# Two-layer decoder on one core: context work of layer 2 behind the first experts, sixteen early maxima, and half of the last sums on PE

## What is computed

```python
x = _layernorm(x + _L0_attn_ref(x, ...))             # ALiBi: 8 heads look back, 8 look forward
x = _layernorm(x + _L0_xattn_ref(x, ctx_768, ...))   # scores clipped to +-10000
x = _layernorm(x + _L0_ffn_ref(x, ...))              # top 2 of 8 gated experts, 704 wide
x = _layernorm(x + _L1_attn_ref(x, ...))             # full attention
x = _layernorm(x + _L1_xattn_ref(x, ctx_768, ...))   # k = ctx @ wk + bk, v = ctx @ wv + bv
x = _layernorm(x + _L1_ffn_ref(x, ...))              # causal latent attention, then top 2 of 8 experts, 512 wide
```

## Time and profile before

| | |
|---|---|
| median of 3 runs | 2091.39 us (2084.49 to 2094.41) |
| profiled execution | 2086.37 us |
| its span in the trace | 2084.6 us |
| PE busy | 1872.3 us (90%), 12192 matmuls |
| DVE busy | 1316.5 us (63%) |
| ACT busy | 1023.2 us (49%) |
| POOL busy | 518.6 us (25%) |
| TensorE's granted clock, mean | 0.94 of 2.4 GHz |

### The profile page before, as it was taken

The page is one execution under the profiler, slowest core; times in us unless marked ns, Lnnn a source line. Parts: engine busy times, 40 slices in busy tenths (PEclk is TensorE's granted clock), DMA queues, the critical chain, the costliest instruction groups (busy, mean ns, idle before and its releaser), DMA issues. The chain is left out here.

```text
span 2084.6 us, 35007 instructions
## 1 busy us (share of the span) xinstructions
PE 1872.3 (90%) x12192; PEld 1089.2 (52%) x12193; DVE 1316.5 (63%) x2305; ACT 1023.2 (49%) x1992; POOL 518.6 (25%) x869
## 2 busy tenths in 40 slices
PE   7899999797689999958999999987988999986992
PEld 4444445342679999934232222253453444476992
DVE  4688874698643333366888888556587888654114
ACT  3266666486212222243677777754643666632333
POOL 3211103333223332212000000222352101043551
PEclk9799999899789999988999999998998999977996
DMA  7554312520911111055221121055046234051224
GB/s 195 134 119 66 49 20 58 133 43 2 373 47 35 35 33 33 30 150 124 39 32 31 32 46 16 1 129 118 11 92 123 43 52 63 2 202 38 71 70 139
DMA packets 98874, 157.94 MB, mean 76 GB/s; under 512 B 31415, under 2 KB 78839, under 8 KB 93559
## 3 DMA queue, kind: packets, MB, share of 16 engines
q1 hardware_dynamic: 86898, 131.55, 27.4%
q0 software_dynamic: 7488, 20.46, 3.1%
q10 hardware_dynamic: 4352, 4.20, 0.6%
HBM read 110.44 MB, written 44.72 MB: 74 GB/s over the span
## 5 line engine op out<-in xcount | busy, mean ns | idle before, releaser
L1871 ACT ACTIVATE arena<-psum 128x512 f32<-128x512 f32 (+1 forms) x1120 | 578.3, 591 | 310.4 <-PE psum L1817 215.9
L1616 DVE TENSOR_REDUCE arena<-psum 128x1 f32<-128x1024 f32 (+7 forms) x384 | 431.0, 1159 | 92.1 <-PE psum L1574 56.7
L1817 PE MATMUL psum<-arena 99*128 99x512 bf16 (+7 forms) x1280 | 369.6, 352 | 8.7 <-DMA arena<-arena 6.3
L1574 PE MATMUL psum<-arena 96*128 96x512 bf16 (+7 forms) x1280 | 355.6, 361 | 15.1 <-SPq L2605 7.3
L2338 PEld LDWEIGHTS psum<-arena 128*128 128x128 f32 x2340 | 278.7, 195 | 7.4 <-ACT arena L2385 3.4
L2338 PE MATMUL psum<-arena 128*128 128x128 f32 x2340 | 280.0, 278 | 2.0 <-ACT arena L2385 1.4
L1835 PE MATMUL psum<-arena 128*32 128x512 f32 (+3 forms) x2560 | 280.7, 538 | 0.7 <-ACT arena L1871 0.7
L2431 DVE COPY arena<-arena 128x1536 f32 (+1 forms) x117 | 97.1, 830 | 287.1 <-PE psum L2338 284.3
L1602 DVE CUSTOM_DVE_ANT_0 arena<-psum,arena 128x1024 bf16<-128x1024 f32 (+3 forms) x224 | 217.4, 1020 | 49.1 <-PE psum L1574 48.9
L1817 PEld LDWEIGHTS psum<-arena 99*128 99x128 bf16 (+1 forms) x1280 | 120.4, 98 | 218.6 <-ACT arena L1871 122.4
L1574 PEld LDWEIGHTS psum<-arena 96*128 96x128 bf16 (+1 forms) x1280 | 109.6, 100 | 184.4 <-DVE arena L1616 47.4
(11 more groups left out here) (207 smaller groups left out, 2301.8 us busy)
## 6 DMA issues: line engine op xcount, KB each, us to landing
arena<-k_parts SPq DMA_DIRECT2D x144, 128.0 KB
q_halves<-arena SPq DMA_DIRECT2D x80, 192.0 KB, 2.9
arena<-q_halves SPq DMA_DIRECT2D x40, 384.0 KB, 4.8
arena<-in_L_ffn_up SPq DMA_DIRECT2D x8, 1408.0 KB, 17.1
arena<-q_halves SPq DMA_DIRECT2D x40, 256.0 KB, 5.3
k_parts<-arena SPq DMA_DIRECT2D x48, 192.0 KB, 3.1
arena<-in_L_ffn_down SPq DMA_DIRECT2D x9, 1024.0 KB, 13.4
arena<-y_rows SPq DMA_DIRECT2D x32, 256.0 KB, 4.0
```

The lines of the kernel that those rows point to most:

```text
L1574: last = nc.tensor.matmul(dst[:, base + lo:base + hi], q[0:rows, qh, h, qb % 4 * P:qb % 4 * P + P], k[0:rows, h, key0 + lo:key0 + hi], sta ...
L1616: nc.vector.tensor_reduce(dst, src, AX.X, ALU.max).then_inc(t("taken"), 1)
L1817: last = nc.tensor.matmul(b[:, at0:at0 + width], kk[0:rows, h, kb * P:kb * P + P], q[0:rows, qh, h, c0:c1], start=True, stop=diag is None)
L1871: nc.scalar.activation(probs[k % at.ahead][:, heads[0]:heads[-1] + 1, c0:c1], bank[st_bank[no % 3]][:, 0:len(heads) * width].rearrange("p ...
```

## The change

It has four parts, and a few costs of the planner.

1. The context part is divided by layer. `t0` keeps layer 1's; layer 2's (two of four key units, four of eight value units) moves into `t3`, with `ctx1_loads` (six DMAs of weights and biases) and two DMAs that load the context rows again. SP issues them behind the row loads of pair 5. PE takes this work after the transposes of pair 3. `vx` is cleared per layer by POOL (128x2048), no longer by DVE, which keeps two small writes. `vx` is stored one layer at a time: 1 MB at the start of `at0`, 1 MB at the start of `at1`.
2. `at0` has all 16 early maxima of job 0, with transpose, split and load, in `t0`.
3. In `xa0` and `xa1` POOL adds the bias of one row tile behind the split of each job. Costs in `CrossAttention.plan` go up, which changes the order of events; in `xa0` nine scores stand between the transpose of a job's maxima and that job's first score in most jobs, ten before.
4. In `t7` the sums of the odd pairs (1, 3, 5, 7) are made by PE in PSUM: per 128 tokens, identity times `x`, then diag(gate1) and diag(gate2) times the gathered rows, three f32 matmuls of 128x256. ACT makes the 16 diagonal tiles of 128x128. DVE takes these pairs' moments from PSUM and ACT normalises from there.

Its core (`@@` lines tell where; new lines of the small helpers that only pass the layer on are left out):

```diff
@@ task costs of a token stage (make_plan)
-                    task("SP", "cload", 0, 4.0, 3.0)
+                if layer is not None:
+                    task("SP", "cload", 0, 5.0, 5.0, ("load", 5))
...
-                        task("SP", "load", p, 1.0, 5.0 if p < 4 else 3.5, ("add", p - 4))
-                    task("DVE", "add", p, 0.75 if source == "proj" else 1.9, 0.15, ("prj", p), ("load", p),
-                         (normed if not norm else "norm", p - 4), ("more", p - 4))
-                    task("DVE", "moments", p, 1.25, 0.15, ("add", p), ("square", p - 4))
+                        task("SP", "load", p, 1.0, 2.8 + 1.4 * p if p < 4 else 5.0, ("add", p - 4), ("sum", p - 4))
+                    if final and p % 2:
+                        task("ACT", "diag", p, 0.9, 0.15)
+                        task("PE", "sum", p, 2.6, 0.2, ("diag", p), ("load", p))
+                        task("DVE", "moments", p, 1.25, 0.15, ("sum", p))
+                    else:
+                        task("DVE", "add", p, 0.75 if source == "proj" else 1.9, 0.15, ("prj", p), ("load", p),
+                             (normed if not norm else "norm", p - 4), ("more", p - 4))
+                        task("DVE", "moments", p, 1.25, 0.15, ("add", p), ("square", p - 4))
...
-                    free = ("att", n_pairs - 1), ("add", n_pairs - 1), ("cmove", 7), ("cbias", 3)
+                    free = ("att", n_pairs - 1), ("add", n_pairs - 1), *context_ends(layer)
...
             def load_rows(sp, p):
                 if p >= 4:
-                    sp.wait_ge(t("r"), p - 3)
+                    summed(sp, p - 4)
...
+            def row_of(u):
+                if on_pe(u // 2):
+                    return bank[u // 4][:, (u % 2) * D:(u % 2) * D + D]
+                return r_tok[:, u % TPB, :]
...
+            def act_diag(act, p):
+                for u in (2 * p, 2 * p + 1):
+                    for k in range(2):
+                        last = nc.scalar.activation(diag_of(u, k), ident, ACT.Copy, scale=gate_w[:, k, u:u + 1])
+                last.then_inc(t("diag"), 1)
...
+            def pe_sum(pe, p):
+                pe.wait_ge(t("diag"), p // 2 + 1)
+                pe.wait_ge(t(f"rows{p % 4}"), 32 * (p // 4 + 1))
+                for u in (2 * p, 2 * p + 1):
+                    nc.tensor.matmul(row_of(u), ident, x_tok[:, u, :], start=True, stop=False)
+                    for k in range(2):
+                        last = nc.tensor.matmul(row_of(u), diag_of(u, k), gathered[:, k, u % TPB, :],
+                                                start=False, stop=(k == 1))
+                last.then_inc(t("prj_ps"), 1)
...
@@ ContextPart
-            def tasks(self, task):
-                task("DVE", "cclear", 0, 4.5, 0.15)
-                for n in range(len(self.kunits)):
-                    task("PE", "ckey", n, 1.1, 0.2, ("cload", 0), ("cbias", n - 2))
+            def tasks(self, task, layer):
+                task("POOL", "czero", 0, 2.2, 0.2)
+                task("DVE", "cclear", 0, 1.5, 0.15, ("czero", 0))
+                for n in (2 * layer, 2 * layer + 1):
+                    task("PE", "ckey", n, 1.3, 0.2, ("cload", 0), ("trx", 3), ("cbias", n - 2))
...
-            def load(self, sp):
+            def load(self, sp, layer):
                 load_context_rows(sp)
-                load_weights(sp, self.wn)
+                if layer == 0:
+                    load_weights(sp, self.wn)
+                else:
+                    for dst, src in ctx1_loads:
+                        sp.dma_start(dst, src, allow_slow_non_contiguous=True).then_inc(sem(f"weights{self.wn}"), 16)
...
-                for l in range(2):
-                    sp.dma_start(vx_scr[l], self.vx[:, l].rearrange("p g b n w -> p (g b n w)"))\
-                        .then_inc(t("vstored"), 16)
...
+                sp.dma_start(vx_scr[l], self.vx[:, l].rearrange("p g b n w -> p (g b n w)"))\
+                    .then_inc(t("vstored"), 16)
...
+            def pool_zero(self, pool, l):
+                nc.gpsimd.memset(self.vx[:, l].rearrange("p g b n w -> p (g b n w)"), 0.0).then_inc(self.t("zero"), 1)
...
-                nc.vector.memset(vx.rearrange("p l g b n w -> p (l g b n w)"), 0.0).then_inc(t("zero"), 1)
...
@@ cross_attention_stage, pool_prog
                 for j in range(1, len(at.jobs)):
                     maxima.pool_split(pool, j)
-                if bias:
-                    add_bias(pool, *bias)
+                    if bias:
+                        add_bias(pool, *bias, (j - 1,) if j < NT - 1 else (j - 1, j))
...
@@ CrossAttention.plan
-                clips.append(on_dve(exps[no], 0.62))
+                clips.append(on_dve(exps[no], 0.7))
...
-                taken.append(on_dve(free["PE"] + 0.2, 0.75))
+                taken.append(on_dve(free["PE"] + 0.2, 0.8))
...
@@ the program
-        at0 = SelfAttention("at0", ("fwd", "bwd"), True, q_halves, k_scr, 8)
+        at0 = SelfAttention("at0", ("fwd", "bwd"), True, q_halves, k_scr)
...
-                     ("v", w["wv"], w["bv"])], w, following=at1)
-        self_attention_stage(at1, (5, W["t4"]["brow"]))
+                     ("v", w["wv"], w["bv"])], w, following=at1, layer=1)
+        self_attention_stage(at1, (5, W["t4"]["brow"]), lambda sp: context.store_values(sp, 1),
+                             rows_free=lambda eng: context.values_stored(eng, 1))
```

More of the change, by code:

```diff
@@ L445, in plan @@
                 free["PE"] = when + (0.25 if tile < HG else 0.5)
-                free["ACT"] = max(free["ACT"], free["PE"] + 0.2, pvs[2 * j - 5] if j > 2 else 0.0) + 0.59
+                free["ACT"] = max(free["ACT"], free["PE"] + 0.2, pvs[2 * j - 5] if j > 2 else 0.0) + (0.7 if kind == "F" else 0.61)
                 exps.append(free["ACT"])
@@ L744, in token_stage @@
         def token_stage(name, wn, source, norm, rms, outs, w, x_out=True, h_rows=None, final=False,
-                        early_sp=None, following=None, between_sp=None, next_weights=True, context=None):
+                        early_sp=None, following=None, between_sp=None, next_weights=True, layer=None):
             def t(n):
@@ L789, in make_plan @@
                 normed = "norm" if rms is None else "rms"
-                if context:
-                    task("SP", "cload", 0, 4.0, 3.0)
+                if layer is not None:
+                    task("SP", "cload", 0, 5.0, 5.0, ("load", 5))
                 for p in range(n_pairs if has_in else 0):
@@ L856, in make_plan @@
                         task("SP", "eload", 0, 1.6, 2.0, ("esplit", 0))
-                if context:
-                    context.tasks(task)
+                if layer is not None:
+                    context.tasks(task, layer)
                 return list_order(tasks)
@@ L862, in ring, with on_pe, summed @@
                 return slice(2 * (p % 4), 2 * (p % 4) + 2)
+            def on_pe(p):
+                return final and p % 2 == 1
+            def summed(eng, p):
+                if final:
+                    eng.wait_ge(t("prj_ps" if on_pe(p) else "r"), p // 2 + 1)
+                else:
+                    eng.wait_ge(t("r"), p + 1)
+            def row_of(u):
+                if on_pe(u // 2):
+                    return bank[u // 4][:, (u % 2) * D:(u % 2) * D + D]
+                return r_tok[:, u % TPB, :]
             def tiles(p):
@@ L934, in sp_prog @@
                     elif kind == "cload":
-                        context.load(sp)
+                        context.load(sp, layer)
                     elif kind == "cstore":
@@ L1002, in pool_prog @@
                         pool_add(pool, n)
+                    elif kind == "czero":
+                        context.pool_zero(pool, layer)
                     elif kind == "cthird":
@@ L1087, in act_prog @@
                         act_norm(act, n)
+                    elif kind == "diag":
+                        act_diag(act, n)
                     elif kind == "xts":
@@ L1099, in act_prog, with diag_of @@
                         context.act_second(act, n)
+            def diag_of(u, k):
+                at0 = rest_base + 128 * (4 * (u // 4) + 2 * (u % 2) + k)
+                return arena[:, at0:at0 + P]
+            def pe_sum(pe, p):
[7 more added lines that the diff above has]
+                last.then_inc(t("prj_ps"), 1)
             def pe_tra(pe, p):
@@ L1173, in banks_free @@
                     pe.wait_ge(t("r"), n_pairs)
-                if context:
-                    context.banks_free(pe)
+                if layer is not None:
+                    context.banks_free(pe, layer)
             def pe_prog(pe):
-                weights_ready(pe, wn)
+                if wn is not None:
+                    weights_ready(pe, wn)
                 for kind, n in plan.get("PE", []):
@@ L1183, in pe_prog @@
                         pe_prj(pe, n)
+                    elif kind == "sum":
+                        pe_sum(pe, n)
                     elif kind == "trx":
```

(24 more changed lines are left out.)

73 lines of the change are left out of this document (44 added, 29 removed).

## The result

| | before | changed |
|---|---|---|
| median, us (runs) | 2091.39 (11) | 2078.8 (11) |
| ratio, 95% interval | | 0.9948 (0.9935 to 0.9961) |
| profiled execution, its span | 2086.4, 2084.6 | 2080.0, 2077.8 |
| PE, DVE, ACT, POOL busy | 1872, 1317, 1023, 519 | 1884, 1300, 1029, 520 |

The change gained 12.6 us of the forecast 24 by the medians, 10.9 by the ratio (8.2 to 13.6). Two single runs of some 3,700 to 3,800 us, one here and one among the experiments, are disturbed executions and stand in no ratio. The two traces differ by 6.8 us only, so part of the 12.6 is not in this pair. For that reason the stages are compared over all traces made, each from one barrier to the next. "Same stage" counts the versions of the changed kernel whose instructions are the same in that stage (for `xa0` and `xa1` those with the changed kernel's order and spread adds).

A forecast was written before the change was run, and what follows sets the result against it. PE bounded `t0`, PE and DVE `xa0`, DVE `t7`; `at0`'s start waited for a DMA. -6 -12 -4 +4.5 -4 = -21.5 gave 2064.9 us from the profile, 2069.9 against the median; taken 2067, range 2050 to 2081.

The forecast's parts named there:

- `t0`, -6: In `t0`, half of PE's context work leaves (-9.1), eight maxima units and a transpose come; the stage ends 6 us earlier.
- the wait for the group's data: In `t0`, early maxima units may stand before their keys land: a wait of up to 3 us, leaving -3.
- `at0`, -12: Start of `at0`: between 15 us gained by an earlier first score and 6.5 to 11.5 by job 2's earlier maxima.
- the start of `at0` is given back: Rival: job 2 waits in full and `t0`'s early units wait for keys; -3 and -7, 2075 us, chance 0.17.
- `xa0`, -4: In `xa0`, -9.5 at the end from spreading POOL's adds, +5.9 in the loop from a slower pace.
- a sign of being wrong: Wrong if `xa0` lengthens, `t3` grows by over 9, or `at0` begins early but ends where it ended.
- The end: End of `xa0`: with two adds instead of sixteen there, the 8.42 us PE wait behind a clip shrinks; about -9.5.
- the pace: Loop of `xa0`: a job takes 7.6 us against 7.15, +0.45 over 13 jobs, +5.9.
- the formula of the prediction: In `xa0`, chain time x 10 / 9 as least job time: (6.3 + 0.4) x 10 / 9 = 7.45 us.
- `t3`, +4.5: `t3` gains the 9.1 us of PE work that `t0` lost; half is taken as paid, the rest falling into gaps.
- `t7`, -4: In `t7`, four pairs' adds leave DVE (-7.2), less a wait of 3 us for PE's last sum.
- gone by the row: End of `xa0`: trusted the profile row showing a clip held through all sixteen adds, over 9 us, not one add.

The follow-up runs named there:

- at0_loaded17: Changed kernel with `at0`'s planner taking the second group's keys as landed 17 us into the stage, not 8; 2080.68 us, 0.9939 of the kernel before.
- number 4: Also written xa_as_before: changed kernel without its cross-attention part (old order, bias adds in one row at the end); 2082.01 us, 0.9962 of the kernel before.
- numbers 5 and 2: Changed kernel with, 5: old order, adds behind the last split, each pair awaiting a clip, 2074.65 us; 2: new order, adds in one row there, 2087.87 us.
- t7_dve: Changed kernel with all sums of `t7` on DVE again; 2077.93 us, 0.9948 of the kernel before.

## Why the prediction was wrong

The direction and the range held, the size did not: 12.6 against 24. By its own steps (forecast, then the difference of the stage means; their sum is uncertain by several us, as `xa0` alone differs by 9 between traces of the same code):

- **`t0`, -6: came as -2.6.** The PE terms held: its work ended 5.4 us sooner, and the wait for the group's data that I had bounded at 3 was 1.24. The step that failed is that PE's end was taken for the stage's end. The moved steps issue on SP too, and the last stores stand behind them, up to 74.43. PE waited 4.53 at the barrier instead of 1.76.
- **`at0`, -12: came as -7.4.** The first score came at 2.1 us, better than the 3 to 5 said. What failed is the next step: I let the second group land 12 to 17 in and saw it as a matter of job 2 alone. It landed at 17.2, while PE had 11 scores and 8 sums ahead of it and had used them up. at0_loaded17 shows that this wait can be moved, not removed: job 2's maxima still leave 42 us in, where 35 to 40 was said. This is the rival "the start of `at0` is given back", with its -3 and -7 for `t0` and `at0` nearly to the number, and I gave it 0.17. Its reason holds for `at0`; for `t0` it named a wait for keys, and that its -3 fits is luck, since the time went at the barrier.
- **`xa0`, -4: by traces +4.6 on the means, by medians -3.2.** The traces are 138.9 in six against 134.3 in four of before's instructions; the runs cannot tell the gain from nothing (number 4), so the sign stays open. I had named a longer `xa0` as a sign of being wrong. The end held: from the fourteenth group to the end of the stage 17.9 us instead of 26.5, and numbers 5 and 2 show it from both sides. The step that failed is the pace, 8.11 (7.84 to 8.41 in all) instead of 7.6. Its chain was read at the last job, 6.3 + 0.4, the shortest of fifteen; on average the way from the transpose to the landed load takes 7.4, before as after. By the formula of the prediction 7.4 x 10 / 9 gives 8.2 a job. Not in the sum at all: most of the waits of 1.7 us drop PE's clock behind them.
- **`t3`, +4.5: +3.0**, in thirteen traces within 0.5. A third of the 9.1 us is paid. PE's busy time in the stage grew by 6.2 only (61.3 to 67.5), its mean clock from 0.86 to 0.88, and half of the 6.2 fell into gaps. In its densest stretch, where the earlier trace rows had 89 matmuls in 29.51 of 30 us at 0.94, PE now runs 113 in less time:

```profile
941.00:971.00 30.00, 29.07 (x113) 15.11 (x112) 26.23 (x34) 9.75 (x16) 7.29 (x8) 1.00 0.45 110
```

- **`t7`, -4: -1.8 by stages, nothing by medians.** The adds went from DVE as said. What failed is the price of the wait: the load of pair 7 waits for PE's sum of pair 3, which stands behind the cold sum of pair 1 (two of its matmuls take 1.06 to 1.19 us, the whole sum 5.3). SP issues the last row loads up to 16.2 us into the stage, up to 12.9 before and 13.4 in t7_dve, and the stage's tail waits for them. The Trainium skill ("TensorE: Matmul & The Clock Gate", What's actually happening) says that PE needs sustained work for its full clock; I had drawn from it that all four sums stay cold. The traces agree with the page and not with what I drew: behind pair 1, which ran cold, pairs 3 and 5 ran warm (two matmuls in 0.59 us), and pair 7 warm behind a wait of 1.66 us, cold behind 3.60.

The rule of the Trainium skill on the shared port ("SBUF — State Buffer", Who interferes with whom: the first has it for its whole instruction) fits the spread adds: the longest of the changed kernel's 80 clips took 1.264 us, its own 0.68 and one add's 0.6. It does not fit adds that follow each other without a pause. Where two stand back to back, at the end of `xa0`, a clip took 1.98 us (at0_loaded17), both adds and itself, and in the row of adds a clip was held for sixteen of them. Removing that row gave the 8 to 9 us that the rule would not have given. I had gone by the row, and that held.

The stages' differences (means of the changed versions less before's, `xa1` left out) sum to -5 with `xa0` at its mean of 138.9 and to -10 with it at its lowest, 133.6; the runs say -8.2 to -13.6. What is left between them is not located. The traced execution of at0_loaded17, with the longest `xa0` of all, took 2091.45 where its median is 2080.68, so the mean of `xa0` may be too high. And no run undoes the first part, the divided context work, alone: what it is worth is read from stages only.

## What to carry to other kernels

When work leaves the engine that bounds a stage, ask what ends the stage at its barrier: here it was the last store's issue, not the last matmul. A gain ahead of a stage's data is worth only what can run before the next load lands; count the work that is queued in front of the first instruction that needs it. A chain that comes back in every job is to be read over all jobs, not at the one place where another wait made you look. Where two engines contend as here, one long row of small operations at the end is worse than the same operations spaced by a wait on the other's progress (0.9962 against 0.9924 for the kernel).

## What the runs showed that I had not expected

A wait of 1.7 us on PE in `xa0` can cost more than itself. In the changed kernel there are five in the loop, and behind four of them the clock was 0.50 to 0.53 for 3 us (0.61 in the 4 us around one of them); behind the first it stayed at 1.00. Behind the one at 463.95 eight matmuls took 1.94 us, 1.07 elsewhere. Behind the 1.62 of xa_as_before the clock was 0.50 for 5 us, and a load that landed 1.5 us later than before's had started it. So a stage with such waits differs by up to 9 us between traces of the same code (133.6 to 142.5), though thirteen traces of `t3` agree within 0.5. The mean clock over `xa0` goes with its length: 0.93 in the shortest of the six traces, 0.88 to 0.89 in the three above 141. Single traces misjudged two parts here, `xa1` (4.6 us of nothing) and `xa0`.
